# Nystrom attention: row sums carried by the product, division with tokens on the partitions, and the shift of the Newton iterate on another engine

## The reference, cut to what matters

```python
kernel1 = softmax(einsum('bhnd,bhmd->bhnm', Q, K_l))     # 16 heads of 8, 64 landmarks
kernel2 = softmax(einsum('bhmd,bhkd->bhmk', Q_l, K_l))
kernel3 = softmax(einsum('bhmd,bhnd->bhmn', Q_l, K))
V = swapaxes(K2, -1, -2) / denom                          # K2 = kernel2
for _ in range(6):
    KV = matmul(K2, V)
    V = matmul(0.25 * V, 13 * I - matmul(KV, 15 * I - matmul(KV, 7 * I - KV)))
SV = matmul(matmul(kernel1, V), matmul(kernel3, Vtok))
out = SV @ w_proj
```

## Time and profile before

| | us |
|---|---|
| median of 3 runs | 1919.78 (1916.09 to 1920.82) |
| the profiled execution | 1921.65 |
| its span, first to last instruction | 1919.2 |
| TensorE matmul busy | 1683.3 (88%) |
| TensorE weight load busy | 1306.7 (68%) |
| VectorE busy | 1506.5 (78%) |
| ScalarE busy | 994.4 (52%) |
| GpSimd busy | 824.8 (43%) |
| mean granted TensorE clock | 0.968 |

### The profile page before, as it was taken

One profiled execution on the slowest core, in us unless ns is written; L12 is line 12 of the kernel. 1 busy time (PEld: TensorE's weight loads), 2 busy tenths in 40 slices (PEclk: granted clock), 3 DMA queues, 4 the chain that ended last, 5 costly groups with the idle time before them and its releaser, 6 DMA issues.

```text
span 1919.2 us, 73934 instructions
## 1 busy us (share of the span) xinstructions
PE 1683.3 (88%) x31945; PEld 1306.7 (68%) x31945; DVE 1506.5 (78%) x3788; ACT 994.4 (52%) x2784; POOL 824.8 (43%) x875
## 2 busy tenths in 40 slices
PE   5999899997999678876999999999999999857897
PEld 4888677775888556665667777767666767635666
DVE  5786577765566699985888888888888888859997
ACT  2444333432344466644666566665566666536664
POOL 2000444442000177753454544454444545427876
PEclk9999899998999899997999999999999999969999
DMA  4000000000000000000000000000000000000001
GB/s 126 1 1 1 2 4 4 4 4 3 1 1 1 1 1 1 1 1 2 4 4 4 3 4 4 4 4 3 4 4 3 4 3 4 3 1 1 23 23 44
DMA packets 14625, 14.92 MB, mean 8 GB/s; under 512 B 1440, under 2 KB 12128, under 8 KB 14304
## 3 DMA queue, kind: packets, MB, share of 16 engines
q1 hardware_dynamic: 11104, 8.83, 1.6%
q10 hardware_dynamic: 3200, 1.37, 0.3%
HBM read 6.01 MB, written 4.19 MB: 5 GB/s over the span
## 4 chain that ended last, share of the span: by engine, by line
PE 59%; DVE 24%; issue 8%; POOL 4%; ACT 4%; DMA 1%; DVEq 0%; POOLq 0%; SPq 0%
PE acc L519 7%; PE acc L496 6%; PE acc L1889 4%; PE acc L1905 3%; DVE arena L1353 3%; PE acc L883 3%; DVE acc L1004 3%; DVE arena L1017 3%; DVE arena L1345 2%; DVE arena L994 2%; PE acc L510 2%; PE acc L1937 2%; PE acc L858 2%; PE acc L1921 2%; PE acc L1839 2%
## 5 line engine op out<-in xcount | busy, mean ns | idle before, releaser
L1041 POOL TENSOR_TENSOR arena<-arena 128x960 f32<-128x960 f32 (+2 forms) x74 | 177.5, 2398 | 312.0 <-DVE arena L1010 216.7
L1686 POOL TENSOR_TENSOR arena<-arena 128x288 f32<-128x288 f32 x192 | 143.6, 748 | 297.8 <-DVE arena L1345 239.9
L1692 POOL TENSOR_TENSOR arena<-arena 128x256 f32<-128x256 f32 x192 | 139.6, 727 | 107.0 <-ACT arena L1572 103.7
L469 ACT ACTIVATE arena<-acc,wib 128x256 f32<-128x256 f32 x256 | 100.5, 475 | 152.9 <-PE acc L510 152.9
L1572 ACT ACTIVATE arena<-acc 128x288 f32<-128x288 f32 x192 | 79.0, 412 | 178.9 <-PE acc L1911 176.6
L1905 PEld LDWEIGHTS acc<-arena 64*64 64x64 f32 x3072 | 110.7, 134 | 68.0 <-DVE arena L1366 65.3
L1905 PE MATMUL acc<-arena 64*64 64x72 f32 (+1 forms) x3072 | 136.7, 225 | 21.8 <-DVE arena L1366 20.0
L1127 PE MATMUL acc<-wguT,arena 128*128 128x352 f32 x256 | 105.2, 494 | 48.1 <-DVE arena L994 47.1
L1889 PE MATMUL acc<-arena 64*64 64x72 f32 x2560 | 116.9, 229 | 32.3 <-POOL arena L1692 32.2
L1889 PEld LDWEIGHTS acc<-arena 64*64 64x64 f32 x2560 | 95.5, 134 | 68.2 <-DVE arena L1359 50.1
L1911 PE MATMUL acc<-arena 64*64 64x72 f32 x3072 | 139.2, 230 | 0.0
(11 more groups left out here) (261 smaller groups left out, 4814.3 us busy)
## 6 DMA issues: line engine op xcount, KB each, us to landing
out_dram<-X SPq DMA_DIRECT2D x3, 1024.0 KB, 5.3
out_dram<-X SPq DMA_DIRECT2D x1, 512.0 KB, 3.2
wi<-in_wiT_dram ACTq DMA_DIRECT2D x1, 256.0 KB, 6.2
wout<-in_woT_dram ACTq DMA_DIRECT2D x1, 256.0 KB, 9.6
out_dram<-X SPq DMA_DIRECT2D x1, 256.0 KB, 2.3
out_dram<-X SPq DMA_DIRECT2D x2, 128.0 KB, 2.6
wqkv<-in_w_qkv_dram ACTq DMA_DIRECT2D x1, 192.0 KB, 6.8
arena<-in_w_down_dram SPq DMA_DIRECT2D x1, 176.0 KB, 4.9
```

The costliest lines, as they stand in the source:

```text
L1041: pool.tensor_tensor(b3(y[k][:, part(u)]), b3(z[k][:, part(u)]), each(small[u % kept][:, 1, blocks(u)]), ALU.mult).then_inc(y_ready, 1)
L1686: pool.tensor_tensor(tm[s][:, :, cols], sq[s][:, group[0], cols], rm[s][:, :, cols], ALU.subtract)\
L1692: pool.tensor_tensor(high[s], sq[s][:, group[1], 0:LM], unit[:, it, :].unsqueeze(1).broadcast_to([P, PG, LM]), ALU.add).then_inc(high_read ...
```

## The change

- `totals`, its ones and the sums of 128x256 go. The weights of `product`, 32 columns per matmul, now hold 16 channels (two heads) and two columns of ones, so that one product gives values and sums. The two halves (t = 0, 1) go to different columns of PSUM and are no longer added up.
- The product then takes this way: ScalarE `evacuate` (copy of 128x512), TensorE `turn_heads` (four transposes), VectorE `invert` (reciprocal of 32 sums per partition) and `divide` (128x256), TensorE `turn_sv` (two transposes), ScalarE `turned_sv` (copy of 128x256), `project`. Its channels come out in another order, so `w_proj` is loaded in 8 pieces of 16 rows.
- `shift` moves from VectorE's queue to GpSimd's.
- Other steps change places in the written order: on VectorE `diagonal`, `kernel2`, `columns`, `largest`, `spread`, `begin_w`, `newton(5, 0)`; on ScalarE `norm`, `exp2`, `masked_queries`, `turned2`, `copy_qk`; on GpSimd `expand_k`; on TensorE `product`, `turn2`, `columns`, `factors` and `turn_w`.

```diff
-        wones = blank_cut(96)
...
+                for m in wd:
+                    for h in range(2):
+                        chain.did(pool.memset(m[h * LM:(h + 1) * LM, :, :, 2 * HD + h], 1.0))
...
-            num = [B[s][1][:, 0:SEQ] for s in R]
-            den = [B[s][1][:, SEQ:2 * SEQ] for s in R]
+            num = [B[s][1].rearrange("p (t n) -> p t n", t=2) for s in R]
+            tok = [B[s][1].rearrange("p (a c) -> p a c", c=32) for s in R]
+            svp = [B[s][1][:, 0:SEQ] for s in R]
...
-                def shift(n, s, it):
-
-                    iterate(dve, n, it, 1)
-                    dve.tensor_tensor(low[s], pm[s][:, group[1], 0:LM],
-                                      eye[:, it, :].unsqueeze(1).broadcast_to([P, PG, LM]), ALU.add).then_inc(low_ready, 1)
...
-                def invert(n, s, j):
-                    dve.wait_ge(den_done, n + 1)
-                    dve.wait_ge(num_done, n + 1)
-                    chain.did(dve.reciprocal(rden[s][:, j * P:(j + 1) * P], den[s][:, j * P:(j + 1) * P]))
+                def invert(n, s):
+                    dve.wait_ge(tok_done, n + 1)
+                    chain.did(dve.reciprocal(rden[s], tok[s][:, :, 2 * HD:2 * HD + 2]))
 
                 def divide(n, s):
-                    dve.wait_ge(num_done, n + 1)
                     chain.settle()
-                    dve.tensor_tensor(svT[s], num[s], rden[s], ALU.mult).then_inc(sv_ready, 1)
+                    dve.tensor_tensor(sv[s].rearrange("p j (a h c) -> p (j a) h c", h=2, c=HD),
+                                      tok[s][:, :, 0:2 * HD].rearrange("p a (h c) -> p a h c", c=HD),
+                                      rden[s].unsqueeze(3).broadcast_to([P, 2 * TPB * NQ, 2, HD]), ALU.mult)\
+                       .then_inc(sv_ready, 1)
...
+                def evacuate(n, s):
+                    act.wait_ge(num_done, n + 1)
+                    act.copy(heads[s], num[s]).then_inc(num_ready, 1)
+
+                def turned_sv(n, s):
+                    act.wait_ge(svT_done, n + 1)
+                    act.copy(svT[s], svp[s]).then_inc(svT_ready, 1)
...
+                def shift(n, s, it):
+
+                    if n < 1:
+                        pool.wait_ge(blank, 1 + 3 * STREAMS + 2 * NITER)
+                    iterate(pool, n, it, 1)
+                    pool.tensor_tensor(low[s], pm[s][:, group[1], 0:LM],
+                                       eye[:, it, :].unsqueeze(1).broadcast_to([P, PG, LM]), ALU.add).then_inc(low_ready, 1)
...
-                            mm = pe.matmul(num[s][quad(q), :], wrow[s][:, q, 32 * t:32 * t + 32], e1[s][:, 2 * q + t, :],
-                                           start=(t == 0), stop=(t == 1), skip_group_check=True)
+                            mm = pe.matmul(num[s][quad(q), t, :], wrow[s][:, q, 48 * t:48 * t + 32], e1[s][:, 2 * q + t, :],
+                                           start=True, stop=True, skip_group_check=True)
...
+                def turn_heads(n, s):
+                    pe.wait_ge(num_ready, n + 1)
+                    for j in range(TPB):
+                        for t in range(2):
+                            mm = pe.transpose(B[s][1][:, (2 * j + t) * P:(2 * j + t + 1) * P],
+                                              heads[s][:, t, j * P:(j + 1) * P], ident[:, :])
+                    mm.then_inc(tok_done, 1)
+
+                def turn_sv(n, s):
+                    pe.wait_ge(sv_ready, n + 1)
+                    for j in range(TPB):
+                        mm = pe.transpose(svp[s][:, j * P:(j + 1) * P], sv[s][:, j, :], ident[:, :])
+                    mm.then_inc(svT_done, 1)
...
-                 (wqkv[:, :], w_qkv), (wproj[:, :], w_proj)]
+                 (wqkv[:, :], w_qkv),
+                 *[(wproj[LM * t + 16 * q:LM * t + 16 * q + 16, :], w_proj[32 * q + 16 * t:32 * q + 16 * t + 16, :])
+                   for t in range(2) for q in range(NQ)]]
```

More of the change, by code:

```diff
@@ L1206, in nystrom @@
             r2 = [cut(2) for _ in R]
-            rden = [cut(SEQ) for _ in R]
+            heads = [cut(2, SEQ) for _ in R]
+            rden = [cut(2 * TPB * NQ, 2) for _ in R]
+            sv = [cut(TPB, D) for _ in R]
             svT = [cut(SEQ) for _ in R]
@@ L1449, in v @@
                         remainder(n, s, 1)
-                        shift(n, s, 1)
+                    if tail:
+                        diagonal(n - 1, o)
                     if head:
@@ L1460, in v @@
                         remainder(n, s, 2)
-                        shift(n, s, 2)
+                    if tail:
+                        invert(n - 1, o)
                     if head:
@@ L1501, in v @@
                         lower1(n, s, 1)
+                        newton(n, s, 5, 0)
                     if fore:
                         landmarks(n + 2, s)
-                    if head:
-                        shift(n + 1, o, 0)
-                    if run:
-                        newton(n, s, 5, 0)
             def a(act):
@@ L1620, in a @@
                         exp2(n + 1, o, 1)
-                    if run:
-                        linear(n, s, 1)
-                    if head:
                         exp2(n + 1, o, 2)
@@ L1626, in a @@
                     if run:
+                        linear(n, s, 1)
+                    if tail:
+                        evacuate(n - 1, o)
+                    if run:
+                        masked_queries(n, s)
                         square(n, s, 2)
+                    if head:
+                        turned2(n + 1, o)
+                    if run:
                         linear(n, s, 2)
-                    if head:
-                        exp3(n + 1, o, 0)
+                    if fore:
+                        norm(n + 2, s)
                     if run:
@@ L1633, in a @@
                     if head:
+                        exp3(n + 1, o, 0)
+                    if tail:
+                        turned_sv(n - 1, o)
+                    if head:
                         exp3(n + 1, o, 1)
-                        turned2(n + 1, o)
                     if run:
                         linear(n, s, 3)
+                        square(n, s, 4)
                     if head:
                         turned_kv(n + 1, o)
-                    if run:
-                        square(n, s, 4)
                     if fore:
@@ L1729, in g @@
                     if run:
+                        shift(n, s, 2)
                         remainder(n, s, 2)
                         raised(n, s, 2)
-                        remainder(n, s, 3)
-                        raised(n, s, 3)
-                        remainder(n, s, 4)
                     if head:
@@ L1737, in g @@
                     if run:
+                        shift(n, s, 3)
+                        remainder(n, s, 3)
+                        raised(n, s, 3)
+                        shift(n, s, 4)
+                        remainder(n, s, 4)
                         raised(n, s, 4)
+                        shift(n, s, 5)
                         remainder(n, s, 5)
@@ L2030, in t @@
                         turned3(n + 1, o)
+                    if tail:
+                        turn_sv(n - 1, o)
                     if run:
```

72 lines of the change are left out of this document (26 added, 46 removed).

## The result

| | before | after |
|---|---|---|
| median of 3 runs, us | 1919.78 (1916.09 to 1920.82) | 1938.35 (1936.95 to 1942.68) |
| the profiled execution, us | 1921.65 | 1936.95 |
| its span, us | 1919.2 | 1935.2 |
| first to last group 1 update (128x288) of the stage, us | 797.53 | 818.56 |

The change makes the kernel slower: ratio 1.011, 95% interval [1.0083, 1.0137], 18.6 us between the medians, against a forecast of 19.8 and a range of 1926 to 1955. Between the two profiled spans the difference is 16.0 us.

The account below looks back on a forecast made before the run. A loop of latencies, no engine, was taken as the bound; 0.57 us per trip over 31 trips (17.7), 1.1 for the last trip and 1.0 at the start gave 19.8 more, median 1939.6, range 1926 to 1955.

Parts of the forecast that it names:

- loop of latencies: Attention stage: handovers between group 1 updates (links 0 to 4, trip 24.98 us) bind; bare loop 4.21, no engine the bound.
- over 4: VectorE, per trip: relieved of six shifts and two reciprocals, less a small reciprocal, over 4 us.
- under 18 us busy: Sign of being right: VectorE busy under 18 us per trip and idle longer, against 21.80 busy before.
- Rival (b): VectorE, not latencies, sets the trip: kernel faster, 1860 us if trips fall to TensorE's 23.04, 1890 at half; chance 0.10.
- Shift, +0.22 a link: Update to cross: shift on GpSimd starts cross 1.43 after the update instead of 1.21, 0.22 us more per bare link.
- Fillers hidden: Links 0 and 1 onward: new transposes, copies and division stay covered, with slacks of 0.26 to 0.3 us.
- Rival (a): Round trips show before cross 2, `both` 2 or `both` 3: 0.3 per trip each, 1949 us, all three 1967; chance 0.14.
- Link 2, -0.22: Third link: shift costs 0.22, but `turn_w` behind `both` removes 0.45 of extra: 4.43 us against 4.65.
- Link 3, +0.20: Fourth link: `begin_w` delays the remainder, cross starts at 1.57: 4.56 to 4.57 us against 4.37; bounds +0.06, +0.35.
- just covered: Link 3, TensorE: `turn_w`, scores and turn_x end at 1.5 us, before cross starts at 1.57.
- Link 4, +0.15: Change of stream: VectorE gains 0.14 at `turned1`, GpSimd's order takes it back, `cube` at 3.83 against 3.67; bounds -0.10, +0.30.
- Start of the kernel, +1.0: Loading `wproj` in 8 pieces adds 3.6 us on ScalarE's queue, exceeding 2.51 idle: +1.1, taken as 1.0; bounds 0, 1.7.

Follow-up runs that it names:

- e6: Kernel before with only the new product, transposes and division, order kept where possible, shift on VectorE, `wproj` in 8 pieces: 1915.14 us, ratio 0.9996 to before.
- e11: As e8, but with shifts 4, 5 and 0 on VectorE too, so all six are there: 1916.96 us, ratio 0.9999 to before.
- e8: Changed kernel with e5 and e9, `diagonal` ahead of the first update, shifts 1, 2, 3 on VectorE, 4, 5, 0 on GpSimd: 1908.26 us, ratio 0.9971 to before.
- e5: Changed kernel with the 8x8 multiply of `largest` on ScalarE instead of VectorE: 1932.68 us, ratio 1.0092 to before.
- e9: Changed kernel with remainder 4 ahead of `begin_w`, and turn_x in another PSUM bank ahead of `start_w`: 1922.33 us, ratio 1.0021 to before.
- e2: Changed kernel in its own order with all shifts back on VectorE, behind each remainder: 1939.65 us, ratio 1.0115 to before.
- e1: Kernel before with only the shift moved to GpSimd, ahead of each remainder: 1935.66 us, ratio 1.0094 to before.
- e7: As e1, with GpSimd's `kernel2` behind the shift of iteration 2 instead of ahead of it: 1933.89 us, ratio 1.0107 to before.
- e10: Changed kernel run again unaltered for a second profile: 1937.52 us (one run).

## Why the prediction was right, and where it was not

**The bound.** Right: a loop of latencies, not VectorE. VectorE was relieved by 2.7 us per trip (not over 4: the held multiply alone gives 0.57 back, and the shifts overlapped their neighbours by 0.1 each) and idles more; e6, which takes only the reciprocals' work away, changes nothing. With that the prediction's "over 4" was too much, and so was "under 18 us busy". Rival (b) fails for the change as made. It has a true core in one place: in link 3 VectorE is full once the rest is put right (e11).

**Shift, +0.22 a link.** The mechanism holds in links 0 and 1, the size was 0.10 to 0.11: both hops were taken too long, 0.24 together against 0.12. In e8, with these shifts back on VectorE, links 0 and 1 are 4.21 again.

**Fillers hidden.** Right for the transposes and the division (e6). Rival (a) came true at the third place that it named, ahead of `both` 3, at its price of 0.3, but not by hops and not through `finish`: `largest`'s multiply was held by GpSimd. The prediction laid out VectorE's steps there with each operation at its own length, whatever GpSimd did beside it.

**Link 2, -0.22.** Measured -0.03. The 0.45 of extra did go, but against it stand 0.13 of shift (4.33 in e5, the multiply on ScalarE, against 4.20) and 0.29 of the held multiply, which was not in the sum: 4.65 - 0.45 + 0.13 + 0.29 = 4.62.

**Link 3, +0.20.** Measured +0.35, the stated upper bound. The step that failed is "just covered": `turn_w`, scores and turn_x issue one after another, 0.37 + 1.08 + 0.37, and end at 1.73, not 1.5. `begin_w` was about right: the remainder behind it starts at 1.12 (1.07 predicted). e9 takes 0.36 back.

**Link 4, +0.15.** Measured -0.05. The step that failed is that GpSimd's order takes the gain back. The five steps were the right ones, but they ran with no gap, each starting 0.04 to 0.05 before the recorded end of the one before, and their chain was no longer the last to end. GpSimd at the change of stream, then TensorE:

```profile
1222.04 0.73 POOL L1698 TENSOR_TENSOR arena<-arena 128x256 f32<-128x256 f32 x1 [1.50 <-DVE arena L1353]
1222.73 0.26 POOL L1684 TENSOR_TENSOR arena<-arena 128x32 f32<-128x32 f32 x1
1222.94 0.62 POOL L1676 TENSOR_TENSOR arena<-arena,rowhot 128x256 f32<-128x256 f32 x1
1223.51 0.73 POOL L1698 TENSOR_TENSOR arena<-arena 128x256 f32<-128x256 f32 x1
1224.19 0.73 POOL L1690 TENSOR_TENSOR arena<-arena 128x256 f32<-128x256 f32 x1
```
```profile
1224.04 1.15 PE L1950 MATMUL acc<-arena 32*128 32x256 f32 x16
1225.11 0.46 PE L1892 MATMUL acc<-arena 64*64 64x8 f32 x10
```

The raised product ends at 1224.92, 3.42 after the update at 1221.50, and `cube` starts at 3.61, behind `turned1`, where 3.83 was predicted: TensorE's chain binds, `turned1` starts at 2.54 against 2.59 before, and so 0.05 of the expected gain of 0.14 is kept. The shift of this link on VectorE instead costs 0.05 to 0.06 (e2, e11).

**Start of the kernel, +1.0.** Measured 0.1: the square root runs at 18.12 against 18.00. ScalarE's queue there:

```profile
10.21 3.90 ACTq L2223 DMA_DIRECT2D wproj<-in_w_proj_dram  x8
...
18.12 0.23 ACT L323 ACTIVATE stat<-stat 128x32 f32<-128x32 f32 x1 [1.75 <-DVE stat L300]
```

The eight pieces took 0.49 each, 3.25 more than the one, yet ScalarE was free only 0.88 later (18.12 - 1.75 = 16.37 against 15.49), since its other loads took less in that execution, and it still idles 1.75 until VectorE's statistics are there. The 2.51 of idle time alone would not have covered 3.25. But it came from an execution with slow loads: with `wproj` in one piece, e1 and e7 have 5.23 and 4.96 of idle time there, and in the ten profiles with eight pieces the idle is 1.44 to 2.31 and the square root comes at 17.90 to 18.47. So the pieces cost about 3 us of ScalarE's idle time, and VectorE sets this point.

**The sum.** 31 x 0.48 = 14.9 us is the regular part, against 17.7 predicted. From first to last update the changed kernel took 21.0 more. The other 6.1 are irregular: the 31 trips are 10.9 longer in all than undisturbed ones, those of before 4.5, and the four links of the last trip, for which the prediction had added 1.1, are 0.3 shorter (18.41 against 18.67). Of the 10.9 the stops of TensorE make up 6.0. Outside the stage the profiled execution was 5.0 shorter (1935.2 - 818.56 against 1919.2 - 797.53), of which 3.2 lie behind the stage. That stretch took 223.3 here, 224.6 in e10, the same kernel, 226.5 before and 223.7 to 232.9 in the other profiles, so it is not put down to the change. So 14.9 - 0.3 + 6.4 - 5.0 = 16.0 between the spans, where 17.7 + 1.1 + 1.0 had been forecast, and 18.6 between the medians. That the total came within 1.2 us is in part luck: the forecast's own terms came to 14.7 (14.9 - 0.3 + 0.1 at the start) instead of 19.8, and 6.4 of irregular trips and -5.1 outside the stage were not in the sum.

**Open.** What stops TensorE is not shown. Most places belong to the program: in e10, 7 of the 11 stops inside the trips come again. The view of waits has 14 in e5, but only 5 in e9, 3 in e6 and 5 in e8, and the mean trip is 0.40 above undisturbed in e5, 0.15, 0.12 and 0.14 in the others; so they depend on the order of steps. What repeats every 11 trips is not shown, and no run separates a cause.

## What to carry to other kernels

Take the busy share of an engine as no bound until the idle time ahead of the step that closes the loop has been read: here 2.7 us per trip less on an engine 87% busy gave nothing, and with the changed order (e2 against the changed kernel) the same move of the shift to GpSimd lengthened link 2 by 0.11 and shortened link 3 by 0.25. When a step goes to GpSimd, list each small VectorE operation that will run beside it and has a waiter, and price it at GpSimd's whole operation, since who starts first decides, here by 0.03 or 0.13 us; whether it is held has to be measured, as large operations were not. And place each moved step by the queue that it enters: filler of 1.04 us ahead of it or behind it cost 0.21 and 0.51.

## What the runs showed of the hardware that was not expected

- A VectorE multiply of 8x8 elements took 0.72 or 0.81 instead of 0.15 when it started with or 0.03 after a GpSimd operation of 0.73 or 0.81, and ended with it. Written as two operations of one tensor and a per-partition scalar it was still held: 0.86 for the pair, and the view of the line has a minimum of 210 ns and a maximum of 870 for one.
- Not all VectorE operations are held: a remainder (two inputs, one of them in PSUM) started 0.40 after GpSimd's raised product of 1224.19 and took 0.45, as in the earlier trace rows:

```profile
1224.59 0.45 DVE L1345 SCALAR_TENSOR_TENSOR arena<-acc,arena 128x288 f32<-128x288 f32 x1
```

- Two large operations hardly hold each other: the remainder on GpSimd has a median of 0.84 beside the old shift, 0.80 after and 0.82 in e8, where three shifts are back on VectorE; the shift itself stayed at 0.41 to 0.42 there. If the one that starts first held the pair to its end, the remainder would have been held until the shift ended (0.19, 1197.79 to 1197.98); it was 0.04 longer. No run separates why.
- Hops between VectorE, GpSimd and TensorE were 0.05 to 0.07 in the shift's path, and GpSimd's operations back to back overlap in the records by 0.03 to 0.05.
- TensorE stops of 0.4 to 1.0 us with nothing to wait for come at seven same places inside the trips in two executions of one program.
